# A stack of four graph layers on one core: half groups as the unit of the pipeline, and score rows spread by DMA through DRAM

## The reference

```python
x = _layernorm(x + _L0_gnn_ref(x, adj, W, a_src, a_dst))       # attention, 4 heads of 64
x = _layernorm(x + _L1_gnn_ref(x, adj, weight, w_ih, ...))     # 3 turns of aggregation and GRU
x = _layernorm(x + _L2_gnn_ref(x, ..., adj, weight, bias))     # relational, relation = adj
x = _layernorm(x + _L3_gnn_ref(x, adj, W, a))                  # attention, 1 head

# attention (L0, per head; L3 alike)
Wh = X @ W
e = leaky_relu(e_src[:, :, None, :] + e_dst[:, None, :, :], 0.2)   # node i down, node j across
alpha = softmax(where(A > 0, e, NEG_INF), axis=2)
H = elu(einsum('bijh,bjhf->bihf', alpha, Wh))

# GRU layer (L1), h = x at first, for each of 3 turns
m = h @ weight[i];  aggr = einsum('bst,bsd->btd', A, m);  h = gru_cell(aggr, h)
```

## Time and profile before

| what | value |
|---|---|
| runs | 2903.97, 2903.30 and 2910.07 us, median 2903.97 |
| the profiled execution | 2902.69 us, its span (first to last instruction) 2900.5 us |
| busy, share of the span | PE 93%, PEld 80%, DVE 75%, ACT 57%, POOL 45% |
| mean granted clock of PE | 0.965 of full |
| DMA | 75.31 MB, 26 GB/s |

### The profile page before, as it was taken

How to read it: one execution, slowest core, us unless ns; L and a number is a source line. 1 busy time by engine, 2 the same in 40 slices (tenths; PEclk the granted TensorE clock), 3 DMA queues, 4 the chain that set the end, 5 groups by cost and what they waited for, 6 DMA issues and landing times. The chain is left out here.

```text
span 2900.5 us, 48930 instructions
## 1 busy us (share of the span) xinstructions
PE 2708.2 (93%) x15577; PEld 2321.7 (80%) x15577; DVE 2175.1 (75%) x5170; ACT 1648.5 (57%) x4164; POOL 1307.8 (45%) x1351
## 2 busy tenths in 40 slices
PE   4589999999999999999999999999999999999944
PEld 2478888888888888888888888888888888888833
DVE  6467778787877878787887878787787878787643
ACT  0445566665666566566656656566666656664422
POOL 0033545444455545445454544445454444545422
PEclk8589999999999999999999999999999999999976
DMA  6000000000000000000000000000000000000000
GB/s 192 19 21 15 21 25 21 23 25 19 23 28 21 28 16 25 26 26 19 25 25 25 20 25 25 17 25 29 21 22 22 25 23 23 25 21 10 10 12 15
DMA packets 97279, 75.31 MB, mean 26 GB/s; under 512 B 6625, under 2 KB 92769, under 8 KB 96993
## 3 DMA queue, kind: packets, MB, share of 16 engines
q1 hardware_dynamic: 77296, 54.28, 6.5%
q10 hardware_dynamic: 19696, 17.44, 1.8%
HBM read 54.93 MB, written 16.78 MB: 25 GB/s over the span
## 5 line engine op out<-in xcount | busy, mean ns | idle before, releaser
L928 PE MATMUL psum<-ag_h,wc_h 128*128 128x512 f32 x1152 | 482.9, 419 | 0.3 <-DVE ag_l L1269 0.3
L928 PE MATMUL psum<-ht_h,whh_h 128*128 128x512 f32 x1152 | 472.7, 410 | 0.0
L928 PE MATMUL psum<-ht_h,whh_l 128*128 128x512 f32 x1152 | 456.6, 396 | 0.0
L928 PE MATMUL psum<-ag_l,wc_h 128*128 128x512 f32 x1152 | 456.3, 396 | 0.0
L928 PE MATMUL psum<-ht_l,whh_h 128*128 128x512 f32 x1152 | 455.2, 395 | 0.0
L928 PE MATMUL psum<-ag_h,wc_l 128*128 128x512 f32 x1152 | 454.2, 394 | 0.0
L1344 POOL TENSOR_SCALAR rstd<-moments 128x2 f32<-128x2 f32 x256 | 95.0, 371 | 743.3 <-DVE moments L1181 742.1
L1398 POOL TENSOR_TENSOR ht<-ht,g_n 128x512 f32<-128x512 f32 x192 | 258.3, 1345 | 271.2 <-ACT g_n L1089 268.0
L1393 POOL TENSOR_TENSOR ht_l<-ht,ht_h 128x1024 fp32r<-128x1024 f32 x64 | 153.9, 2404 | 290.6 <-DVE ht_h L1295 290.6
L928 PEld LDWEIGHTS psum<-ht_h,whh_l 128*128 128x128 f32 x1152 | 216.7, 188 | 52.3
L928 PEld LDWEIGHTS psum<-ag_h,wc_l 128*128 128x128 f32 x1152 | 216.3, 188 | 51.9
(11 more groups left out here) (151 smaller groups left out, 7178.9 us busy)
## 6 DMA issues: line engine op xcount, KB each, us to landing
adj_i<-in_adj_dram SPq DMA_DIRECT2D x128, 128.0 KB, 2.1
x_in<-in_x_dram SPq DMA_DIRECT2D x64, 256.0 KB, 2.8
out_dram<-out_t ACTq DMA_DIRECT2D x64, 256.0 KB, 2.1
adj_g<-in_adj_dram SPq DMA_DIRECT2D x32, 256.0 KB, 3.3
hh_raw<-in_L_gnn_w_hh_dram SPq DMA_DIRECT2D x1, 768.0 KB, 7.3
ih_raw<-in_L_gnn_w_ih_dram SPq DMA_DIRECT2D x1, 768.0 KB, 10.9
wl_raw<-in_L_gnn_weight_dram SPq DMA_DIRECT2D x1, 768.0 KB, 12.4
wrs<-in_L_gnn_weight_dram SPq DMA_DIRECT2D x1, 768.0 KB, 10.1
```

What stands on the lines that cost most here:

```text
L928: last = mm(dst, s, m, start=(first and k == 0), stop=(last_part and k == len(flat) - 1))
```

## The change

The unit of the pipeline is now a half group of 4 graphs, k = 0 to 31, with two units each. One table, HALF, is the order of one block, and block t is laid out for t = -2 to 34. The first argument of a step in the table is relative: step(-1, ...) in block t belongs to half group t - 1. `placed` leaves out steps whose half group doesn't exist. So there are no separate parts for the beginning and the end. In block t stand: the GRU turns of half t-1 (second part of turn 1, turn 2) and of half t (turn 0, first part of turn 1), the first layer for halves t+1 and t+2, and the relational and last layers of halves t-1, t-2 and t-3.

In place of att_scores on PE there is att_rows: one transpose per graph of all its e_dst columns (128x4 in the first layer, 128x1 in the last), 2 per unit, to 4 (or 1) partitions of PSUM. ACT copies these rows to SBUF (first_rows, last_rows), SP stores them to a small tensor in DRAM (first_kept: 2 graphs x 4 heads x 128, 4 KB; last_kept: 1 KB), and, when that has landed, loads them back with a broadcast to 128 partitions (att_spread, first_scores 128x512, twice per unit; last_scores 128x256, once). ACT adds e_src in place, in SBUF. The rest of the softmax is as it was. x1 has three buffers of half a group and gru_keep is gone; x3 has two buffers.

```diff
+         "pre_pen": 1, "pre_rows": 2, "post_rows": 1, "pre_t": 2, "pre_pt": 2, "pre_hn": 1, "pre_y": 1,
...
-gru_agg(0,0,0)  next.pre_load(0)  last.post_load(0)  next.att_xt(pre,0)
...
+HALF = """
+gru_rzh(-1,1,1)  gru_new(-1,1,0)
...
+gru_hn(0,1,1)  gru_nodes0(1)  att_rows(pre,2,0)  att_spread(pre,2,0,0)  gru_turn0(1,0)  gru_turn0(1,1)
...
-def make_segments(groups):
-    start = [s for s in pre_steps(0) if s] + [("gru_load", 0, (0,))] + flat(between_groups(0, None, 0))
-    end = flat(between_groups(1, 0, None)) + [s for s in post_steps(0) if s]
-    return [Segment(start, 0, 1), Segment(trip(True, False), 0, 1),
-            *[Segment(trip(False, False), g, g + 1) for g in range(1, groups - 1)],
-            Segment(trip(False, True), groups - 1, groups), Segment(end, groups - 1, groups)]
...
+def placed(step, t, halves):
+
+
+    name, a = step[0], step[1:]
+    kind, a = (a[:1], a[1:]) if name.startswith("att") else ((), a)
+    k = t + a[0]
+    if not 0 <= k < halves:
+        return []
+    if name.startswith("gru"):
+        return [(name, k) + a[1:]]
+    return [(name,) + kind + (2 * k + a[1],) + a[2:]]
+
+
+def program_order(halves):
+
+    return [s for t in range(-2, halves + 3) for step in half_steps(HALF) for s in placed(step, t, halves)]


...
+            def att_rows(kind, u):
+                L, i = LAY[kind], slot(kind + "_rows", "att_rows", kind, u)
+                sp.wait_ge(L.rows_ready, u + 1)
+                for spread in L.spread:
+                    after(sp, spread, 16 * (u + 1 - SLOTS[kind + "_rows"]))
+                sp.dma_start(L.kept[i].rearrange("q h n -> h q n"), L.rows[i][:]).then_inc(L.rows_kept, 16)
+
+            def att_spread(kind, u, q):
+
+                L, i = LAY[kind], slot(kind + "_rows", "att_rows", kind, u)
+                ti = take(sp, kind + "_t", "att_spread", kind, u, q)
+                sp.wait_ge(L.rows_kept, 16 * (u + 1))
+                n = L.heads if kind == "pre" else 2
+                kept = L.kept[i][q:q + 1].rearrange("a h n -> a (h n)") if kind == "pre" else L.kept[i].rearrange("q h n -> h (q n)")
+                sp.dma_start(L.scores[ti][:, 0:n, :].rearrange("p h n -> p (h n)"), kept.broadcast_to([P, n * P])).then_inc(L.spread[q], 16)
+
...
-            def att_scores(v, step, kind, u, q):
-
-                L, i = LAY[kind], take(pe, v, step, "light")
-                w = slot(v, step, "att_wh", (kind, u, 0), "wh")
-                pe.wait_ge(L.wh_ready, nth(v, step, 8, 2 * u + (q if kind == "pre" else 1)))
-                cells = [(q, h) for h in range(L.heads)] if kind == "pre" else [(0, 0), (1, 0)]
-                for k, (g, h) in enumerate(cells):
-                    col = D + L.heads + h
-                    last = turn(LIGHT[:, i, k * P:(k + 1) * P], wh[w][:, g, col:col + 1].to_broadcast([P, P]), ident[:])
-                last.then_inc(L.sc_psum, 1)
...
+            def att_rows(kind, u):
+
+                L, i = LAY[kind], take(pe, "light", "att_rows", kind, u)
+                w = slot("wh", "att_wh", kind, u, 0)
+                pe.wait_ge(L.wh_ready, 2 * u + 2)
+                for q in range(2):
+                    last = turn(LIGHT[0:L.heads, i, q * P:(q + 1) * P], wh[w][:, q, D + L.heads:D + 2 * L.heads], ident[:])
+                last.then_inc(L.rows_psum, 1)
...
+            def att_rows(kind, u):
+
+                L, i = LAY[kind], slot("light", "att_rows", kind, u)
+                r = take(act, kind + "_rows", "att_rows", kind, u)
+                act.wait_ge(L.rows_psum, u + 1)
+                f(L.rows[r][:].rearrange("h q n -> h (q n)"), LIGHT[0:L.heads, i, 0:2 * P], ACT.Copy).then_inc(L.rows_ready, 1)
+
+            def att_scores(kind, u, q):
+
+                L = LAY[kind]
+                w = slot("wh", "att_wh", kind, u, 0)
+                ti = slot(kind + "_t", "att_spread", kind, u, q)
+                act.wait_ge(L.spread[q], 16 * (u + 1))
                 cells = [(q, h) for h in range(L.heads)] if kind == "pre" else [(0, 0), (1, 0)]
                 for k, (g, h) in enumerate(cells):
-                    f(L.scores[ti][:, k, :], LIGHT[:, i, k * P:(k + 1) * P], ACT.Identity,
-                      bias=wh[w][:, g, D + h:D + h + 1]).then_inc(L.shifted, 1)
-
-            def att_prob(v, step, kind, u):
+                    f(L.scores[ti][:, k, :], L.scores[ti][:, k, :], ACT.Identity, bias=wh[w][:, g, D + h:D + h + 1]).then_inc(L.shifted, 1)
+
+            def att_prob(kind, u):
...
-            def gru_keep(v, step, b):
-                dve.wait_ge(s_x1n[b], nth(v, step, 2, 1))
-
-                after(dve, s_fin_y, nth(v, step, 4, 2 * b + 1) + -4)
-                nc.vector.tensor_copy(x1r[b][:], x1n[b][:]).then_inc(s_x1r, 1)
```

More of the change, by code:

```diff
@@ L163 @@
-gru_agg(0,0,1)
-gru_hn(0,0,0)  last.rel_split(0)
-gru_rzh(0,0,0)  last.rel_adjt(0)  last.rel_mask(0)  last.gru_fin(1,0)  next.att_wh(pre,0,0)  next.att_wh(pre,0,1)
-        next.att_scores(pre,0,0)
-gru_r(0,0,0)
-gru_z(0,0,0)  gru_nodes0(1)  last.rel_h1(0)
-gru_in(0,0,0)  last.gru_norm(1,0)  next.att_scores(pre,0,1)
-gru_hn(0,0,1)  last.rel_y1(0)  last.rel_rest(0)  last.gru_fin(1,1)  gru_load(1)  next.att_prob(pre,0)
-gru_rzh(0,0,1)  gru_keep(1)  last.rel_norm(0)  gru_turn0(1,0)  gru_turn0(1,1)  next.att_pt(pre,0,0)  gru_n(0,0,0)
@@ L232 @@
-gru_in(1,2,0)  next.att_res(pre,3)  last.att_pt(post,3,0)  next.gru_turn0(0,0)  next.gru_turn0(0,1)  gru_n(1,2,0)
-        last.att_pv(post,3)  gru_new(1,2,0)
-gru_hn(1,2,1)
-gru_rzh(1,2,1)  last.att_exp(post,3)  gru_norm(0,1)  last.att_res(post,3)
-gru_r(1,2,1)
-gru_z(1,2,1)  gru_n(1,2,1)
-gru_in(1,2,1)  next.att_norm(pre,3)  last.att_norm(post,3)  last.att_store(post,3)  gru_new(1,2,1)
+    if name == "att_norm" and a[0] == "pre" and a[1] % 2 == 0:
+        out.append("x1")
+    return out
+HALF = """
@@ L239, with half_steps @@
+gru_in(0,1,0)  rel_split(-1,0)  att_norm(pre,1,1)  att_norm(post,-2,0)  rel_adjt(-1,0)  gru_n(0,1,0)  rel_mask(-1,0)
+gru_hn(0,1,1)  gru_nodes0(1)  att_rows(pre,2,0)  att_spread(pre,2,0,0)  gru_turn0(1,0)  gru_turn0(1,1)
 """
-def trip(first, last):
+def half_steps(text):
     steps = []
-    for word in TRIP.split():
+    for word in text.split():
         name, args = word[:-1].split("(")
-        off = 1 if name.startswith("next.") else -1 if name.startswith("last.") else 0
-        if not (first and off < 0) and not (last and off > 0):
-            steps.append((name.split(".")[-1], off, tuple(int(a) if a.isdigit() else a for a in args.split(","))))
-    return steps
@@ L265, in number_uses @@
-def number_uses(segments):
-    before = {r: 0 for r in SLOTS}
-    for seg in segments:
-        seg.uses, seg.takers = {}, {r: [] for r in SLOTS}
-        count = {r: 0 for r in SLOTS}
-        for s in seg.order:
-            for r in takes(s):
-                seg.uses[(r,) + s] = count[r]
-                seg.takers[r].append(s)
-                count[r] += 1
-        seg.before, seg.per = dict(before), count
-        for r in SLOTS:
-            assert count[r] % SLOTS[r] == 0 and before[r] % SLOTS[r] == 0, r
-            before[r] += count[r] * (seg.end - seg.first)
+        steps.append((name,) + tuple(a if a in ("pre", "post") else int(a) for a in args.split(",")))
@@ new lines, in take, with t_slots @@
+        def take(eng, resource, *step):
+            n = uses[(resource,) + step]
+            if n >= SLOTS[resource]:
+                eng.wait_ge(*last_read(resource, *takers[resource][n - SLOTS[resource]]))
+            return n % SLOTS[resource]
+        def walk(eng, shares):
+            for step in order:
+                if step[0] in shares:
+                    shares[step[0]](*step[1:])
+        def t_slots(kind, u):
+            return [(slot(kind + "_t", "att_spread", kind, u, q if kind == "pre" else 0), h if kind == "pre" else q, q, h)
```

858 lines of the change are left out of this document (371 added, 487 removed).

## The result

The changed kernel takes **2930.14 us** (median of 4 runs, 2928.96 to 2931.16), the kernel before beside it 2903.64 (2902.59 to 2910.07): ratio 1.0086, 95% interval 1.0069 to 1.0104. It is 0.9% slower. The forecast was 2818 us, range 2785 to 2870, faster with a chance of 0.88: wrong in sign and in size.

What follows compares the result with a forecast made beforehand. PE's issue bounds the middle, chains through all engines the ends. Start 122.4 + PE work (2592 - 11 - 13) + idle 30 + gaps 22 + end 74 = 2816 us, plus 2.2 and 1.3, given as 2818; range 2785 to 2870.

Steps and rivals of the forecast that it cites:

- the transposes: PE in the middle: 384 transposes go at 0.109 us each, narrow ones priced alike, saving 41.9 us.
- the ends: Start and end: first aggregation at 122.4 us, 74 us behind the last gate product; 30 and 51 us gained.
- the cover of the trip: Between rows and transposes back: 15.1 us of PE work at the shortest hides the DRAM round trip, leaving 5.0 us.
- landing under 3 us: Sign of a right forecast: the spreads' loads from DRAM land in under 3 us.
- the middle's idle time: PE's waits in the middle: about 1.0 us per half, 30 us over 30 halves, bounds 0.2 and 3 per half.
- the slack at the head of a half: Rows to aggregation's end: 11.3 us of PE work against 7.5 of copy, trip and shifts; ACT waits at times, PE not.
- other new waits that cost more than 3 us per half: Unspecified new waits in the middle, over 3 us per half; chance 0.14 together with rival (c).
- rival (c): ACT's wait for the last layer's spread: far longer DRAM trip, 2985 us at 14 us; shared chance 0.14.
- Rival (a): Middle: eight-shift burst ahead of ag_h raises PE's idle from 1.0 to 2.3 us per half, 2857 us; chance 0.13.

Runs made afterwards that it cites:

- quarter_spread: Changed kernel with the first layer's spread loading only one head's row of four, 64 KB instead of 256 KB per load: 2930.74 us.
- shifts_late: Changed kernel with unit 1's eight first-layer shifts and masks moved behind the aggregation and the adjacency's turn at the head of a half: 2904.49 us.
- low_spread_late: Changed kernel with x_l and x + bias placed on DVE by its queue, shifts and masks behind the aggregation, x1's norm and x_in load earlier: 2857.40 us.
- pool_small: Changed kernel with POOL's x_l and x + bias cut to 16 of 256 columns, the rest left out: 2827.15 us.
- pe_turns: Changed kernel with scores broadcast by PE transposes again, without small rows or the trip through DRAM, half groups kept: 3082.26 us.
- turns_mended: low_spread_late with PE transposes instead of rows and spread, the edit of pe_turns in that mended order: 2928.57 us.

## Why the prediction was wrong

**Right: the transposes.** The narrow ones run at 0.1 us each, as priced: around the two at 1405.93 a gate product and the second one behind them start 0.68 us apart (1405.71 and 1406.39), where two steps from one gate product to the next, 0.235 each, make 0.47. That leaves 0.21 for the two. Around the two transposes of adj_f with 128 columns at 1362.80 it is 0.68 as well. With the two POOL operations cut, a half takes 81.8 us with 0.8 of waits, so 81.0 of issue; the forecast had 81.0.

**Right: the ends.** 124.3 and 71.9 us against 122.4 and 74.

**Right: the cover of the trip.** First, store, spread and shift in the same head of a half (SP's issues; median landings of the run, KB and us):

```profile
1366.36 0.28 SPq L610 DMA_DIRECT2D first_kept<-first_rows  x1
1367.68 0.80 SPq L619 DMA_DIRECT2D first_scores<-first_kept  x2
...
first_scores<-first_kept SPq DMA_DIRECT2D x128, 256.0 KB, 4.2
x_in<-in_x_dram SPq DMA_DIRECT2D x64, 256.0 KB, 3.9
```

The spread is issued 1.3 us after the store and takes 4.2, so 5.5 us from the rows where I had 4.9 (bounds 3 and 7); "landing under 3 us" was wrong. By the median both spreads have landed at some 1372.4 (an estimate), and ACT's shifts start at 1376.60. quarter_spread confirms it: a load a quarter as large changes nothing. The 4 KB store into DRAM had landed within the 1.3 us, since the spread is issued only then; over 1000 us of the middle SP waits for that store 23 times, 18.1 us in all and 1.4 at the most.

**Wrong: the middle's idle time.** I took "the idle time of before, 1.95 us per trip, about 1.0 per half", as if it belonged to the work. It belongs to an order, and the order was new. 3.7 us per half instead of 1.0, and 0.7 of issue more, make about 3.4 x 30 = 102 of the 112 us; where the other 10 lie was not traced. My upper bound of 3 us per half had no row behind it either.

**Wrong: the slack at the head of a half.** "The tightest place: about 11.3 us of PE work from the rows to the end of the aggregation, against 0.4 + 4.9 + 2.2 (eight shifts) = 7.5. So ACT waits at times, PE does not." The sum counts the DMA and the shifts, and forgets what else stands ahead of the shifts: last_hn and with it DVE's queue. At the head of a half that was 1.81 us of ACT's waiting for last_hn, 2.07 us of DVE behind hn_l and twice 1.07 us of DVE at the masks, and PE answered with 1.07 and 1.14 us. No DVE operation in the prediction is priced by what POOL does beside it. The prediction says that gru_load "delays one gru_n by some 2.5 us" and stops there; it follows POOL's queue, but not DVE beside POOL. The trace of before showed the effect, in the very stretch that I used: beside POOL's hn_l at 148.29 stands

```profile
148.79 2.55 DVE L1262 CAST ht_h<-ht 128x512 fp32r<-128x512 f32 x1
151.98 0.57 DVE L1262 CAST ht_h<-ht 128x512 fp32r<-128x512 f32 x1
```

the same cast, 2.55 us beside hn_l. Alone it takes 0.42 (at 176.59, for one); the 0.57 of the second row is a short hold-up too, for it ends 0.28 us after POOL's first_pen (151.14, 1.13 us long). I put this stretch into the sum as a whole and did not ask where the new order would lay such pairs.

**The rivals.** The case that came true, "other new waits that cost more than 3 us per half", shared 0.14 with rival (c), and no mechanism stood behind it. Rival (a) named the right place (shifts in a burst ahead of ag_h) and the right answer of PE, at a price of 1.3 us per half; the burst is part of it, as shifts_late shows with 26 us, but POOL is the larger part. Rival (c), the long trip, was the named loser and played no part in the middle.

**Two slips in the sums.** 2816 + 2.2 + 1.3 is 2819.5, not 2818. And by the terms of (c) with its ends (32 us for each us above 9.9, 4 for each above 4.9) a round trip of 11.7 us undoes the gain, not 12.8. Neither bears on the miss.

**What stays open.** low_spread_late needs 83.0 us per half and pool_small 81.8. Its waits are 1.3 us per half against 0.8, its issue is 81.7 against 81.0, and the latter I can't explain. How much of pool_small's 103 us is DVE's standing still and how much POOL's shorter queue is not separated. An order without the four waits that are left was not found. How pe_turns' 152 us split between the held banks and POOL is known only in part: in the mended order the same edit costs 71.

## What to carry to other kernels

When a change rearranges a tuned pipeline, its idle time can't be carried over from before: for each place where the bottleneck engine will need something, follow the queue of the engine that delivers it, the whole way. Look in the trace for one instruction with two durations; the longer one has a neighbour, here a POOL operation on two SBUF tensors, and in a new order it may get that neighbour at the worst place. And where PE's waits move on when one is removed, the cause lies ahead of all of them.

## What the runs showed of the hardware

In the changed kernel three kinds of DVE operation, all with inputs in SBUF, took longer beside a POOL operation on two SBUF tensors of 512 or 1024 columns: the mask (128x128) 1.36 us instead of 0.29 beside x_l and x + bias, the cast ht_h (512) 1.52 instead of 0.42 beside x + bias, the state update (512, two inputs) 2.76 instead of 0.69 beside hn_l. They end 0.15, 0.29 and 0.55 us after POOL's end, each some 0.14 less than it takes alone, as if they stood ready. It was so five times out of five for each of these pairs between 1270 and 1660 us. Two operations beside POOL did not take longer: ht_l, which has an input in PSUM (at 1369.08, 0.69 us beside POOL's state difference of 1.47), and g_hn beside a POOL operation with a single tensor (at 1375.41, 0.68 us beside last_pen of 1.08). It is not the single tensor that decides: beside POOL's cast adj_f (266.63, 0.85 us), which reads one tensor too, g_hn at 267.15 took 0.88 us and ended 0.55 after it. What does decide stays open, and what makes DVE stand still there is not shown by these runs.

Loads took longer with the spreads than without: from issue to landing the median for x_in was 3.9 us in the changed kernel against 2.8 before, 3.2 in quarter_spread, and 2.8 again in turns_mended, which has no spread.
